# Graph attention over 4096 nodes on one core: projecting three of the four row groups between the products of chunk 0

## The reference

```python
h = jnp.maximum(_layernorm(x, axis=-1), 0.0)
Wh = h @ W
a1, a2 = (a[:Fout, 0], a[Fout:, 0])
e = (Wh @ a1)[:, None] + (Wh @ a2)[None, :]
e = jnp.where(e > 0, e, 0.2 * e)
e = jnp.where(adj > 0, e, -9e15)
attention = jax.nn.softmax(e, axis=1)
return x + jax.nn.elu(attention @ Wh)
```

## Time and profile before

| | |
|---|---|
| median of three runs | 246.54 us |
| profiled execution | 246.57 us |
| its span | 244.7 us |
| PE busy | 227.1 us (93%) |
| DVE busy | 196.3 us (80%) |
| ACT busy | 156.4 us (64%) |
| POOL busy | 59.0 us (24%) |
| DMA | 71.92 MB, mean 294 GB/s |

### The profile page before, as it was taken

One profiled execution on the slowest core, in us unless ns is written; L12 is line 12 of the kernel. 1 busy time (PEld: TensorE's weight loads), 2 busy tenths in 40 slices (PEclk: granted clock), 3 DMA queues, 4 the chain that ended last, 5 costly groups with the idle time before them and its releaser, 6 DMA issues.

```text
span 244.7 us, 8257 instructions
## 1 busy us (share of the span) xinstructions
PE 227.1 (93%) x3736; PEld 221.2 (90%) x3736; DVE 196.3 (80%) x259; ACT 156.4 (64%) x139; POOL 59.0 (24%) x48
## 2 busy tenths in 40 slices
PE   6969999599999899999999999999999999999780
PEld 2759999599999899999999999999999999999770
DVE  4999897536777898889887988898879888988935
ACT  3688836697799999935996687029976772000052
POOL 3647037896000070300000550000003800040000
PEclk9997999999999999999999999999999999999996
DMA  6999999999998999999999999999999200020002
GB/s 223 364 389 387 387 388 387 387 360 333 337 336 299 343 396 387 387 387 387 398 386 386 386 388 385 386 386 361 384 390 386 79 3 0 3 88 3 0 3 91
DMA packets 36521, 71.92 MB, mean 294 GB/s; under 512 B 1282, under 2 KB 1924, under 8 KB 36484
## 3 DMA queue, kind: packets, MB, share of 16 engines
q1 hardware_dynamic: 35520, 69.74, 78.7%
q10 hardware_dynamic: 964, 1.64, 1.8%
HBM read 69.27 MB, written 2.10 MB: 292 GB/s over the span
## 4 chain that ended last, share of the span: by engine, by line
PE 78%; DVE 10%; POOL 4%; issue 4%; ACT 2%; DMA 1%; DVEq 0%; POOLq 0%; ACTq 0%
PE acc L834 21%; PE acc L835 21%; PE acc L836 21%; PE mask_t L817 11%; DVE words L610 3%; POOL v L330 2%; POOL val L333 2%; DVE stats L547 1%; DMA x_sb<-in_x_dram 1%; PE acc L805 1%; PE acc L796 1%; ACT v L508 1%; DVE wh_sb L573 1%; DVE hp L718 1%; DVE num L709 1%
## 5 line engine op out<-in xcount | busy, mean ns | idle before, releaser
L610 DVE SCALAR_TENSOR_TENSOR words<-g_row,gq_word,mask_t 128x1024 f32<-128x1024 f32 x128 | 161.2, 1278 | 36.6 <-PE acc L836 18.7
L834 PE MATMUL acc<-val,words 128*128 128x129 f16 x992 | 170.6, 220 | 1.2 <-DVE num L618 0.9
L835 PE MATMUL acc<-val,words 128*128 128x129 f16 x992 | 170.6, 220 | 0.0
L836 PE MATMUL acc<-val,words 128*128 128x129 f16 x992 | 170.6, 220 | 0.0
L420 ACT ACTIVATE mask<-raw,step_bias 128x2048 uint8<-128x2048 int32 x63 | 121.9, 1993 | 28.8 <-DVE x_sb L626 17.7
L834 PEld LDWEIGHTS acc<-val,words 128*128 128x128 f16 x992 | 97.1, 98 | 1.5 <-DVE words L610 1.0
L835 PEld LDWEIGHTS acc<-val,words 128*128 128x128 f16 x992 | 97.1, 98 | 0.1
L836 PEld LDWEIGHTS acc<-val,words 128*128 128x128 f16 x992 | 97.1, 98 | 0.0
L817 PE MATMUL mask_t<-ident_b,mask 128*128 128x128 bf16 x512 | 34.5, 222 | 1.4 <-ACT mask L420 1.4
L817 PEld LDWEIGHTS mask_t<-ident_b,mask 128*128 128x128 bf16 x512 | 30.6, 99 | 1.5 <-ACT mask L420 1.5
L358 POOL TENSOR_TENSOR hp<-num,rz 128x1024 f32<-128x1024 f32 x3 | 5.7, 1897 | 106.3 <-DVE rz L621 106.3
(11 more groups left out here) (90 smaller groups left out, 131.9 us busy)
## 6 DMA issues: line engine op xcount, KB each, us to landing
raw<-in_adj_dram SPq DMA_DIRECT2D x64, 1024.0 KB, 14.0
x_sb<-in_x_dram SPq DMA_DIRECT2D x8, 256.0 KB, 5.8
out_dram<-x_sb ACTq DMA_DIRECT2D x3, 512.0 KB, 7.1
out_dram<-x_sb SPq DMA_DIRECT2D x2, 128.0 KB, 1.8
out_dram<-x_sb SPq DMA_DIRECT2D x1, 192.0 KB, 1.9
w_sb<-in_L_gnn_W_dram ACTq DMA_DIRECT2D x1, 64.0 KB
out_dram<-x_sb SPq DMA_DIRECT2D x1, 64.0 KB, 1.6
a_sb<-in_L_gnn_a_dram ACTq DMA_DIRECT2D x1, 1.0 KB
```

The source lines that it names most:

```text
L610: nc.vector.scalar_tensor_tensor(words[:, q], g_row[:, c * CHUNK:(c + 1) * CHUNK], gq_word[:, 1, t:t + 1], maskt_bytes[:, u % 2, q // 2, : ...
L834: nc.tensor.matmul(acc_tile(t), high, val[:, tile, 0, 0:V], start=first and t % PT == 0, stop=False, skip_group_check=True)
L835: nc.tensor.matmul(acc_tile(t), high, val[:, tile, 1, 0:V], start=False, stop=False, skip_group_check=True)
L836: last = nc.tensor.matmul(acc_tile(t), low, val[:, tile, 0, 0:V], start=False, stop=False, skip_group_check=True)
```

## The change

- **Order of the projections.** Only group 0 is projected before the first product. Groups 1, 2 and 3 are projected between the products of chunk 0 (products are counted w = 4u + q). `moments` is split into `means` and `variances`. Products of chunk 0 wait for the scalars and values of their own block.
- **PSUM banks.** The banks of the sums hold products from w = 0 on, so the later projections go through two banks of `mask_t` that the second unit's mask takes later, and through `aux` (`turned_bank`, `projected_bank`).
- **Values.** DVE and ACT make the high values of block 0, POOL its low ones; POOL alone makes those of blocks 1 to 7 (`values`: product, cast, difference).
- **Loads.** x and adj are interleaved: blocks 0, 1 of x, unit 0 of adj, blocks 2, 3 of x, unit 1, and so on.
- **ACT's order.** `to_bytes(0, 0, 1)` stands ahead of the exponentials of group 0. Each group has its own exponentials. The squares and the row copies of groups 2 and 3 move to chunks 1 and 2.
- **Spreading.** Group 1 is spread in unit 5 of chunk 0, groups 2 and 3 in chunks 1 and 2.
- **First mask of a chunk.** `turn(1, 0)` stands ahead of the last unit of chunk 0 instead of within it.
- **The end.** The last unit's first word is multiplied like any other; the other three go tile by tile. DVE makes `num` and `rz` of all three banks first, then the results.

The core of the diff (PE's queue, then DVE's, ACT's and POOL's):

```diff
+            keep_awake(3, mask_t[:, 0, 0, :])
+            turn(0, 0)
             spread_words(0, 0)
             spread_words(0, 1)
+            keep_awake(6, aux)
             for u in range(U):
+                if u % 2 == 0:
+                    pe.wait_ge(z_ready, u // 2 + 1)
                 if u == 0:
+                    pe.wait_ge(vl_first, 1)
+                else:
+                    pe.wait_ge(vl_ready, u)
+                if u == U - 1:
+                    turn(0, u + 1)
                 for q in range(BT):
                     product(0, u, q)
+                    w = u * BT + q
+                    if w == 0:
+                        turn_x(2)
+                        turn_x(3)
+                    if w == 1:
+                        for k in range(3):
+                            project(1, k)
+                    if w in (20, 22):
+                        spread_words(1, (w - 20) // 2)
+                    if q == (2 if u == 0 else 1) and u < U - 1:
                         turn(0, u + 1)
+                    if w in (5, 6):
+                        turn_x(w - 1)
+                    if w in (7, 8, 9):
+                        project(2, w - 7)
+                    if w in (11, 12):
+                        turn_x(w - 5)
+                    if w in (14, 15, 16):
+                        project(3, w - 14)
...
+                            if c < C - 1 and u in (1, 2) and q == 1:
+                                spread_words(c + 1, u - 1)
...
             def last_product():
-                pe.wait_ge(words_ready, N // P * C)
+                product(C - 1, U - 1, 0)
                 for t in range(CT):
-                    for q in range(BT):
+                    for q in range(1, BT):
+                        if t == 0:
+                            pe.wait_ge(words_ready, BT * (C * U - 1) + q + 1)
...
+            for w in range(U * BT):
+                u, q = w // BT, w % BT
+                weights(0, u, q)
+                if w == 0:
+                    variances(2, CT, 2 * CT)
+                if w == 3:
+                    for k in range(3):
+                        keep_projected(1, k)
+                    row_halves(4)
+                    link(row_halves(5))
+                    means(3, 2 * CT, 3 * CT)
+                if w == 4:
+                    variances(3, 2 * CT, 3 * CT)
+                if w == 5:
+                    make_words(1, 2, 6)
+                    split_weights_sums(1, 2, 6)
+                if w == 8:
+                    row_halves(6)
+                if w == 9:
+                    link(row_halves(7))
+                    means(4, 3 * CT, 4 * CT)
+                    variances(4, 3 * CT, 4 * CT)
+                if w in (10, 11, 12):
+                    keep_projected(2, w - 10)
...
             rectify(1)
+            to_bytes(0, 0, 1)
+            exponentials(0, 1)
+            first_high_values()
+            row_copy(0, 0)
+            row_copy(0, 1)
             centre(2)
             centre(3)
+            to_bytes(0, 1, 0)
             rectify(2)
             rectify(3)
+            to_bytes(0, 1, 1)
+            exponentials(1, 2)
+            to_bytes(0, 2, 0)
             centre(4)
             centre(5)
+            to_bytes(0, 2, 1)
             rectify(4)
             rectify(5)
+            to_bytes(0, 3, 0)
+            to_bytes(0, 3, 1)
+            exponentials(2, 3)
             centre(6)
             centre(7)
+            to_bytes(0, 4, 0)
             rectify(6)
+            to_bytes(0, 4, 1)
             rectify(7)
+            to_bytes(0, 5, 0)
+            to_bytes(0, 5, 1)
+            exponentials(3, 4)
+            for u in (6, 7):
+                for k in range(2):
+                    to_bytes(0, u, k)
+                    if u == 6:
+                        row_copy(1, k)
...
+            def values(b):
+                tt = slice(b * BT, (b + 1) * BT)
+                nc.gpsimd.tensor_tensor(v32[:, b % 2, 0:BT], wh_sb[:, tt, 0:F], dv[:, tt].unsqueeze(2).broadcast_to([P, BT, F]), ALU.mult
+                                        ).then_inc(v32_ready, 1)
+                pool.wait_ge(v32_ready, b)
+                nc.gpsimd.tensor_copy(val[:, tt, 0, 0:F], v32[:, b % 2, 0:BT]).then_inc(vh_ready, 1)
+                pool.wait_ge(vh_ready, b)
+                nc.gpsimd.tensor_tensor(val[:, tt, 1, 0:F], v32[:, b % 2, 0:BT], val[:, tt, 0, 0:F], ALU.subtract).then_inc(vl_ready, 1)
```

More of the change, by code:

```diff
@@ L249, in load_raw @@
                 sp.dma_start(raw[:, n % RING, k * BT:(k + 1) * BT], adj_v[n // U, k, n % U]).then_inc(raw_in[n % RING][k], 16)
[L251 to L259, removed]
+            for n in range(C * U):
+                if n < G:
+                    load_x(2 * n)
+                    load_x(2 * n + 1)
                 for k in range(2):
-                    if n == RING and k == 0:
+                    if (n, k) == (RING, 0):
                         sp.wait_ge(first_bytes, 1)
@@ L349, in _ @@
-            for g in range(2, G):
-                pool.wait_ge(wh_sum, g - 1)
-                nc.gpsimd.tensor_tensor(total, total, wh_sb[:, group(g), 0:F], ALU.add).then_inc(wh_sum, 1)
+            pool.wait_ge(vh_first, 1)
+            nc.gpsimd.tensor_tensor(val[:, 0:BT, 1, 0:F], v32[:, 0, 0:BT], val[:, 0:BT, 0, 0:F], ALU.subtract).then_inc(vl_first, 1)
+            centre(2)
+            centre(3)
+            inverse_deviation(2, CT, 2 * CT)
+            values(1)
+            centre(4)
@@ new lines, in _ @@
+            centre(5)
+            inverse_deviation(3, 2 * CT, 3 * CT)
+            pool.wait_ge(z_ready, 2)
+            values(2)
+            values(3)
+            centre(6)
+            centre(7)
+            inverse_deviation(4, 3 * CT, 4 * CT)
+            pool.wait_ge(z_ready, 3)
+            values(4)
+            values(5)
+            nc.gpsimd.tensor_tensor(hp[:], wh_sb[:, group(0), 0:F], wh_sb[:, group(1), 0:F], ALU.add).then_inc(wh_sum, 1)
+            pool.wait_ge(wh_sum, 1)
+            nc.gpsimd.tensor_tensor(hp[:], hp[:], wh_sb[:, group(2), 0:F], ALU.add).then_inc(wh_sum, 1)
@@ L491, in _ @@
             for c in range(1, C):
-                for u in range(6):
+                for u in range(1 if c == 1 else 0, 6):
                     for k in range(2):
                         to_bytes(c, u, k)
+                    if c < C - 1 and u in (4, 5):
+                        row_copy(c + 1, u - 4)
+                    if c == 2 and u < G:
+                        square(u)
                 tail(c - 1)
@@ L630, in _ @@
                 link(row_halves(b))
-                moments(b, b * BT, (b + 1) * BT)
+                means(b, b * BT, (b + 1) * BT)
+                variances(b, b * BT, (b + 1) * BT)
                 centre(b)
+            dve.wait_ge(raw_in[0][0], 16)
+            nc.vector.tensor_scalar(mask[:, 0, 0:BT], raw[:, 0, 0:BT], 0, None, ALU.is_gt).then_inc(first_bytes, 1)
+            for k in range(3):
+                keep_projected(0, k)
+            make_words(0, 1, 3)
+            first_values()
@@ L633, in _ @@
+            split_weights_sums(0, 1, 3)
             row_halves(2)
             link(row_halves(3))
[L635 to L656, removed]
-            dve.wait_ge(grow_ready, 2)
[L658 to L661, removed]
@@ L853, in last_product, with keep_awake @@
                         last.then_inc(acc_done, 1)
-            def keep_awake(n):
+            def keep_awake(n, bank):
                 for _ in range(n):
-                    nc.tensor.matmul(mask_t[:, 0, 0, :], ident_b[:], ident_b[:].unsqueeze(1).broadcast_to([P, BT, P]), start=True, stop=True)
-            keep_awake(8)
+                    nc.tensor.matmul(bank, ident_b[:], ident_b[:].unsqueeze(1).broadcast_to([P, BT, P]), start=True, stop=True)
+            keep_awake(8, mask_t[:, 0, 0, :])
             turn_x(0)
@@ L872, in _ @@
                 project(0, k)
-            keep_awake(4)
-            turn_x(2)
-            turn_x(3)
-            keep_awake(2)
+            keep_awake(3, mask_t[:, 0, 0, :])
+            turn(0, 0)
             spread_words(0, 0)
             spread_words(0, 1)
-            for k in range(3):
-                project(1, k)
-            turn_x(4)
-            turn_x(5)
-            pe.wait_ge(grow_ready, 2)
-            pe.wait_ge(first_bytes, 1)
-            turn(0, 0)
-            for k in range(3):
-                project(2, k)
```

206 lines of the change are left out of this document (83 added, 123 removed).

## The result

Seven runs of the changed kernel took 247.50 to 248.78 us, median 247.88, against 246.54 before: a ratio of 1.0062, 95% interval 1.0045 to 1.0080 (the ratios aren't taken from the two medians alone, whose quotient is 1.0054). The change makes the kernel 0.6% slower; forecast were 245.4 us and faster. The profiled execution took 247.50 us, its span is 245.7.

The account below looks back on a forecast made before the run. PE was taken to bound the kernel from its first product on. Start -8.45, moved work +7.95, pauses 5.1 against 4.0 and tail -1.75 summed to -1.15 from 246.57: 245.4 us, range 243.4 to 247.6.

Parts of the forecast that it names:

- The bound: Whole kernel: PE is the bound nearly throughout from the first product on, at 1.36 us a product.
- The start: Before the first product: unit 0's second half lands at 11.4 us, first product at 18.4, 8.5 earlier.
- PE's work behind the first product: Chunk 0: six `turn_x` (2.65) and three groups of projections (5.3) move behind the first product, +7.95 us.
- PE's pauses: Chunk 0: waits of PE for DVE and ACT sum to 5.1 us, against 4.0 before.
- 0.7 at `turn_x(6)`: Chunk 0: PE waits 0.7 us for ACT's exponentials and centre(6), after group 2 is kept at 42.7.
- 1.4 before turn(0, 4): Chunk 0: PE waits 1.4 us while ACT finishes centre(7), two halves to bytes and a rectify.
- 0.8 ahead of p4 and p5: Chunk 0, products 4 and 5: PE waits 0.8 us for words held by turn(0, 1), statistics and `variances(3)`.
- turn(0, 6), turn(0, 7) and the boundary: Late chunk 0: PE waits 1.35 and 0.45 us for ACT at the turns, about 0.15 at the chunk's boundary.
- POOL: Values of blocks 1 to 7: 3.3 us a block, cast 1.2, at least 5.6 us of room, so no cost.
- The tail: Last unit and results: -1.75 us, of which 1.36 is PE ending earlier; ends -1.3 and -2.2.
- The one on the other side: Start: the half lands late, at 14.1, giving 248.1 us; loss begins with a landing after 12.5; chance 0.11.
- The clock's case: Start: PE's clock drops to half after a pause, first products 1.4 us later, 246.8 us; chance 0.18.

Follow-up runs that it names:

- e3: The changed kernel with DVE keeping bank 0 of group 2 right behind block 7's statistics, ahead of means, variances and word 10: 246.01 us, 0.9978 of the kernel before.
- e10: The changed kernel with an extra POOL copy of 128 x 512 elements behind the difference in each block of values: 247.80 us, 1.0056 of the kernel before.
- e9: The changed kernel run again without any edit, as a yardstick: 247.85 us, 1.0057 of the kernel before.
- e6: The changed kernel with an extra POOL copy of 128 x 512 elements ahead of the cast in each block of values: 249.47 us, 1.0122 of the kernel before.
- e1: The changed kernel with group 0's exponentials ahead of `to_bytes(0, 0, 1)` on ACT and PE's spreads ahead of turn(0, 0): 246.10 us, 0.9978 of the kernel before.
- e8: The changed kernel with exponentials first, group 2's bank kept earlier, bytes in ACT's idle stretches, group 0 kept before half 0's conversion: 241.08 us, 0.9780 of the kernel before.

## Why the prediction was wrong, by its steps

- **The bound.** Right: PE from the first product on, with the same 1.36 us a product, no pause behind 86.65, and the spreads neither gain nor loss.
- **The start.** The mechanism was right: bytes behind the landing, exponentials at the landing plus 2.0, the first product 7.0 behind it. The landing was mis-sized. It was issued at 2.3 and landed at 12.3 instead of 11.4: 274 GB/s x 12.3 = 3.37 MB had moved, at a slower pace than the 286 that I took from before, and its lag was 0.68 MB, not 0.57. **+1.0 us.** In the nine profiles with this order of loads the landing lies between 11.7 and 13.1, so that a single profile can't place it closer.
- **PE's work behind the first product.** The projections cost 5.8, not 5.3, counted from start to start: the first bank of each group, and every bank that follows a product, took some 0.06 more than its share of 1.78. **+0.5.**
- **PE's pauses.** Here is the step that failed. The prediction has group 2 kept behind w10 to w12, at 42.7, and its sum treats this only as a delay for ACT. The kernel has more: all banks of groups 2 and 3 are `aux`, so `project(2, 1)` must wait until DVE has kept bank 0 behind statistics and w10. That wait, 1.68 and a drain, was not in the sum; e3 removed it and took 1.9 us off. The last bank was kept at 45.1, so ACT began on it later too. The 0.7 at `turn_x(6)` and the 1.4 before turn(0, 4) came as one wait, 1.0 and a drain before `turn_x(7)`, which also goes through `aux` and waits for ACT's rectify. Together these places cost 3.0 instead of 2.1. The 0.8 ahead of p4 and p5 was 0.7 (0.3 of it listed); turn(0, 6), turn(0, 7) and the boundary came as worked out (1.22 with its drain against 1.35, 0.39 with its drain against 0.45, 0.17 against 0.15). **+0.9.**
- **POOL.** Right that it has room, e10 shows it. The cast took 0.61 us, not 1.2: the row of 2.79 us, an operation with a constant, was the wrong neighbour. The Trainium skill, GPSIMD Engine Reference, Engine selection, has one-input operations roughly at line rate; the cast's 0.61 bears that out better than the 2.79. By the Trainium skill, GPSIMD Engine Reference, Elementwise, with 1.03 cycles an element, the cast is an estimated 0.44 us at 1.2 GHz; the 0.6 that the prediction worked out from it is a slip that happened to fit. The row of 2.45 us was misread as well. DVE's statistics had ended before it began; three of its four tiles took 0.37 us, and the third 1.40, beside two DVE instructions over 128 x 512 elements with two SBUF inputs (16.32 to 17.60). Neither changes the sum.
- **The tail.** -2.1 instead of -1.75, the one term that came out better: **-0.3.**
- **The rivals.** The one on the other side was right in kind: from a landing at 12.5 on the change loses, it said; with 0.9 more in pauses and 0.5 in work, and 0.3 less in the tail, the point was nearer 11.4, where the forecast had the half, and it landed at 12.3. That the rival's 248.1 lies close to the 247.9 measured is luck: it had the half at 14.1. The clock's case did not decide, but it has a price. In the profile of the changed kernel the granted clock was 1.00 throughout the start. In e9's it was 0.59 on average from 14 to 18 us, the turn took 1.89 us instead of 1.07, and the first product came 7.7 us behind a landing at 12.2 instead of 7.0: 0.6 us, less than the 1.4 forecast, as the low clock fell ahead of p0. That run took 247.93 against the 247.50 of the other profile.

## What to carry to other kernels

When a step is moved between other work, write down for each of its instructions which buffer it needs and who empties it: three projections through one bank made a ring with DVE's queue, and no engine's busy time showed it. An engine that idles before a wait while work that could run already stands behind the wait is the cheapest gain there is: three such reorderings turned +0.6% into -2.1%. A wait for a load belongs behind everything that doesn't need the load.

## What the hardware showed that I had not expected

A short DVE instruction with two SBUF inputs that meets a POOL instruction can be held until that one ends. Beside e6 there are more cases. Here are e1's means of group 1 on DVE (0.17 us when alone), which end at 15.80, with POOL's difference at 15.77:

```profile
14.61 1.16 POOL L338 TENSOR_TENSOR val<-v,val 128x512 f16<-128x512 f32 x1 [6.27 <-ACT val L420]
...
14.93 0.87 DVE L569 TENSOR_TENSOR twice<-stats 128x8 f32<-128x8 f32 x1
```

In e8 the same pair took 0.44 us and ended at 15.73 and 15.70. It doesn't take two inputs on POOL: in e10 the second instruction of the variances (0.19 us in the changed kernel) met POOL's copy, which has one, and ended at 39.68, the copy at 39.66:

```profile
39.01 0.65 POOL L333 COPY neg<-v 128x512 f32<-128x512 f32 x1
...
39.21 0.47 DVE L576 SCALAR_TENSOR_TENSOR spread_sq<-stats 128x8 f32<-128x8 f32 x1
```

And not every meeting does it. POOL's power has two SBUF inputs and takes 1.65 us, but DVE's two-input instructions beside it are not held, here in the changed kernel:

```profile
29.34 1.65 POOL L314 TENSOR_TENSOR half_rstd<-var,minus_half 128x8 f32<-128x8 f32 x1 [0.58 <-DVE var L577]
...
30.65 0.17 DVE L602 TENSOR_TENSOR gq_word<-gq,gq_hi 128x16 f16<-128x16 f32 x1
```

The words, whose second tensor is in PSUM, show nothing of it: 1.278 us on average before and after. The first cases agree with the Trainium skill, GPSIMD Engine Reference, Specifications, by which POOL shares its SBUF interfaces with DVE and contends with DVE instructions that have two SBUF inputs. The rows add that the short one then waited for the end of the long one, and that the power is an exception, whose reason no run here shows.
